# Cross-attention scores as three products of high and low halves

## The chip, the cores and the metric

The kernel runs on one core of one Trainium2 chip. The metric is device time in microseconds (us): the median of the runs of one launch of the whole program. In the views PE is TensorE (matmuls), PEld its weight loads, DVE is VectorE, ACT is ScalarE, POOL is GpSimd, SP is SyncE (it issues most of the DMAs).

## The reference, cut to what matters

One transformer block with cross-attention and a mixture of experts, on 8 sequences of 112 tokens of width 512 (896 tokens), each with a context of 375 rows. The self- and cross-attention parts share one shape of computation:

```python
q  = ln(fp8_linear(ln(x), wq));   k  = ln(fp8_linear(ln(x), wk));   v = fp8_linear(ln(x), wv)
core = softmax(q k^T / sqrt(128)) v           # 16 heads, 8 groups of keys and values, 112 x 112 scores
qx = ln(fp8_linear(ln(x), wqx))               # 16 heads of width 128
kx, vx = split(ctx @ w_kv_x);  kx = ln(kx)    # 8 groups of keys and values from the context
xout = softmax(qx kx^T / sqrt(128)) vx        # 112 x 375 scores for each head: the cross scores
y = fp8_round(concat(core, xout)) @ wproj     # then the gate, the residual, and 8 experts, 2 for each token
```

The change is in `qx kx^T`, and in buffers around it.

## The kernel before, in words

**Work and tiles.** The 16 heads are cut into 4 groups of 4 heads (`GP`, written `g`, 0 to 3). In each group there are 8 sequences (`u`, 0 to 7). A position `(g, u)` stands for the attention of sequence `u` in group `g`: 32 positions. The tokens come in only 7 tiles of 128 rows (`TJ`), so positions with `u` = 7 project no queries and keys of their own (`has_tile`). For one position and its 4 heads there are 4 cross scores: `score_cross(t, h)`, h = 0 to 3, each a matmul of 112 stationary columns (queries `qxT`) by 375 moving columns (context keys `kxT`), in f32. A pair of heads shares one set of keys: h = 0, 1 use `kxT[:, 0]`, h = 2, 3 use `kxT[:, 1]`. An f32 matmul is two records in the trace. Other big matmuls hold f32 numbers cut into a rounded high half and a low rest (type fp32r, tiles `..._hi` and `..._lo`), and each such matmul is one record.

**Steps.** `passes` runs one `step(s, t, ...)` after the other. In a step TensorE makes the six projections of position `s` and the attention of the position `t` before it, interleaved in an order written out by hand for every engine; each engine runs its own list in order and waits on semaphores. There are ordinary steps (`s` with `u` = 1 to 6), the `"new"` steps (`s` = `(g, 0)`, a new group), and `last_step` (`s` = `(g, 7)`, `t` = `(g, 6)`), with lists of their own. The lists of an ordinary step:

- TensorE (L902): project 0, turn 0, turn 1, project 1, turn 2, turn 3, project 2, score_self, score_cross 0 and 1, turn 4, project 3, turn_self, turn_cross 0, score_cross 2, turn_cross 1, score_cross 3, project 4, outputs 0, turn_cross 2 and 3, project 5, outputs 1. `turn` transposes queries and keys into PSUM (turn 1 the cross queries, turn 3 and 4 the two sets of context keys); `turn_cross` transposes exponentials. `turn_cross` 1 needs the bank that VectorE's `take_self` frees (`bank_free`, L802).
- ScalarE (L695): turned 0 (from PSUM to `qT`), take 0, turned 1 (to `qxT`, L647 and L648), turned 2, c_high 0, turned 3 (to `kxT`, L640), take 1, c_high 1, exp_self, exp_cross 0 and 1 (L664), turned 4, take 2, c_high 2, take 3, exp_cross 2 and 3, and so on. `c_high` (L581) rounds a third of the context to `c_hi`.
- VectorE (L1171): sums 0 (L1078), max_self (L1093), max_cross 0 and 1 (L1107), norm_self (L1099, L1101), norm_cross 0 and 1 (L1113, then L1115 twice), take_self (L1121), sums 1, take_cross 0 (L1126), max_cross 2, ...
- GpSimd (L532): c_low 0 (L529: `c_lo = c_raw - c_hi`, as soon as ScalarE has made that `c_hi`), rstd 0 (L516, L523), c_low 1, rstd 1, c_low 2, ...
- SyncE (L437): the loads of the context of a coming position, and the store of a finished position's rounded results (`Results.store`).

In the steps before and at a change of group VectorE and ScalarE also cut the next group's weights (`w_low` L434, `w_low_half` L971, `w_high` L576).

After the attention comes the output projection and the experts (`projected_experts`), which the change touches only through the tile `results`.

Of the kernel before, what the change touches and what calls it, by code (L numbers as in the profile page):

```python
# [25 lines left out]
P = 128  # L26
# [3 lines left out]
KB = D // P  # L30
# [150 lines left out]
class Results:  # L181
# [3 lines left out]
    def __init__(self, c, sb, sem, catd):  # L185
        self.catd = catd
        self.held = sb(c, "results", [P, 4 * 8 * T], BF16)
        *self.y, self.e, self.cat = (self.held[:, k * 8 * T:(k + 1) * 8 * T] for k in range(4))
        self.ya_done = sem(c, "ya_done")
        self.rnd = sem(c, "rnd_chain")  # L190
        self.ct_done = sem(c, "ct_done")
        self.stored = sem(c, "cat_out")
# [13 lines left out]
    def rounded(self, v, t):  # L206
        v.wait_ge(self.rnd, 3 * t + 2)
        y = self.y[t % 2]
        v.tensor_tensor(y[:, :], y[:, :], self.e[:, :], ALU.add).then_inc(self.rnd, 1)
        v.wait_ge(self.rnd, 3 * t + 3)  # L210
        v.wait_ge(self.stored, 16 * (t + 1))
        v.tensor_tensor(self.cat[:, :], y[:, :], self.e[:, :], ALU.subtract).then_inc(self.ct_done, 1)

    def store(self, sp, t):
        sp.wait_ge(self.ct_done, t + 1)
        sp.dma_start(self.catd[t], self.cat[:, :]).then_inc(self.stored, 16)
# [60 lines left out]

def tr_no(pos, n):

    return TR0 + 77 * pos[0] + 10 * pos[1] + n + 1 - (0 if has_tile(pos) else 3)  # L280
# [11 lines left out]
def attention(nc, c, sb, ps, sem, x, vecs, scalars, smooth, ctxT, wproj, catd, vec, scal, gate,  # L292
# [22 lines left out]
    sqx = sb(c, "sqx", [P, 2 * HD], BF16)  # L315
    re = sb(c, "re", [P, 4, 2, P], BF16)
    st = sb(c, "st", [P, TJ, 6])
# [6 lines left out]
    smr = sb(c, "smr", [P, GP, 8])  # L324
    work = sb(c, "work", [P, HP * TC + 2 * NC * 256 + NC * HP * T])
    pcross = work[:, 0:HP * TC].rearrange("p (h c) -> p h c", h=HP)
    at = HP * TC
# [4 lines left out]
    ss = sb(c, "ss", [P, 16])  # L332
    va = sb(c, "va", [P, 16])
    rs = sb(c, "rs", [P, 16])
# [3 lines left out]
    kxT = sb(c, "kxT", [P, 2, TC])  # L338
# [51 lines left out]
    sx_rdy = sem(c, "sx_rdy")  # L390
    mx_done = sem(c, "mx_done")
# [45 lines left out]
    def _(sp):  # L437
# [18 lines left out]
        sp.dma_start(smr[:, :, :], smooth).then_inc(vec_in, 16)  # L456
# [9 lines left out]
        for gp in range(GP):  # L466
# [19 lines left out]
            with sp.Fori(2, B) as b:  # L486
                for k in range(NC):
                    load_c(s0 + b, b, k)
                results.store(sp, s0 + b - 2)

    @block.gpsimd
    def _(pool):
# [4 lines left out]
        pool.wait_ge(pool_self, 3)  # L497
# [60 lines left out]
    def _(act):  # L558
# [71 lines left out]
        def turned(t, n):  # L630
# [8 lines left out]
            if n >= 3:  # L639
                act.activation(kxT[:, n - 3, :], turn_bank(n)[:, 0:TC], ACT.Identity, bias=b,  # L640
                               scale=w).then_inc(t_done, 1)
                return
# [17 lines left out]
        def exp_cross(t, h):  # L660
            act.wait_ge(mx_done, 4 * (lin(t) + 1) + h + 1)
            act.wait_ge(tr_rdy, tr_no(before(t), 6 + h))
            act.wait_ge(nx_done, 4 * lin(t) + h + 1)
            act.activation(pcross[0:T, h, :], p_cross[0:T, h % 2, 0:TC], ACT.Exp,  # L664
                           bias=nmax[0:T, 4 + h:5 + h], accum_out=lsum[0:T, 4 + h:5 + h]).then_inc(ex_done, 1)
# [29 lines left out]
        def step(s, t, g, change, k):  # L695
# [11 lines left out]
            if not A and Q: turned(t, 4)  # L707
            if A: take(s, 1)
            if A: c_high(s, 1)
# [3 lines left out]
            if A and Q: turned(t, 4)  # L713
# [42 lines left out]
    def _(pe):  # L756
# [18 lines left out]
        def project(s, j, g=None):  # L775
# [13 lines left out]
            else:  # L789
# [62 lines left out]
        def turn_cross(t, h):  # L852
            pe.wait_ge(nx_done, 4 * (lin(t) + 1) + h + 1)
            bank_free(t, 6 + h)
            for k in range(NC):
                m = pe.transpose(p_tr[0:CT, 1 - h % 2, k * T:(k + 1) * T], pcross[0:T, h, k * CT:(k + 1) * CT],  # L856
# [21 lines left out]
        def last_step(s, t):  # L878
# [5 lines left out]
            project(s, 3)  # L884
            turn(t, 3)
# [16 lines left out]
        def step(s, t, g, change, k):  # L902
# [45 lines left out]
    def _(v):  # L948
# [75 lines left out]
        def constants():  # L1024

            link(v.reciprocal(smi[:, :, :], smr[:, :, :]))
# [62 lines left out]

        def max_self(t):  # L1090
# [19 lines left out]
        def norm_cross(t, h):  # L1110
# [4 lines left out]
            v.tensor_scalar(pcross[0:T, h, :], pcross[0:T, h, :], linv[0:T, 4 + h:5 + h], None,  # L1115
# [22 lines left out]
        def last_step(s, t, g, change):  # L1138

            if change == "keys": w_low_half(g, 1, 0)  # L1140
            max_self(t)
# [5 lines left out]
            norm_cross(t, 1)  # L1147
            take_self(t)
# [22 lines left out]
        def step(s, t, g, change, k):  # L1171
# [885 lines left out]
```

## Time and profile before

| what | value |
|---|---|
| median of 3 runs | 1150.24 us (1149.46 to 1151.94) |
| the profiled execution: its time | 1153.25 us |
| the profiled execution: span, first to last instruction | 1151.5 us |
| TensorE busy | 1092.3 us, 95% of the span |
| VectorE busy | 779.6 us, 68% |
| ScalarE busy | 698.5 us, 61% |
| GpSimd busy | 505.0 us, 44% |
| granted TensorE clock, mean | 0.977 |

The attention takes the first 797 us or so, the output projection and the experts the rest. A timeline row reads: start in us from the span's first instruction, length in us, engine, line, operation, output tile <- input tiles, shapes, count of merged instructions, and in brackets the engine's idle time before it with what ended it.

### The profile page before, as it was taken

What the parts mean: (1) busy time and instruction counts of PE and PEld (TensorE: products, weight loads), DVE (VectorE), ACT (ScalarE), POOL (GpSimd) and SP (SyncE); (2) the same over time, 40 slices, a digit from 0 to 9 for tenths busy, and PEclk for the clock granted to TensorE, in tenths of its full rate; (3) what the DMA queues carried; (4) which work ended last, traced back from release to release, by engine and by line L of the source; (5) the groups of instructions that cost most, each with busy time, mean ns of one, the idle gap of its engine ahead of it and who ended that gap; (6) DMA issues with size and microseconds to landing.
All of it is one profiled execution on the core that took longest, in us unless ns stands there. A gap on an engine that the chain in (4) does not pass through costs nothing. (4 is left out here: it accounts for less than half of the span.)

```text
span 1151.5 us, 19576 instructions
## 1 busy us (share of the span) xinstructions
PE 1092.3 (95%) x5681; PEld 896.0 (78%) x5681; DVE 779.6 (68%) x1569; ACT 698.5 (61%) x2034; POOL 505.0 (44%) x576
## 2 busy tenths in 40 slices
PE   4599999999999999999999999998999789999996
PEld 3488788888888788888888888886888667777885
DVE  7998986977776887777697766677454884655000
ACT  7668878666878856888867656762231324334432
POOL 3445565445544454445544544542000225565432
PEclk8799999999999999999999999998999889999999
DMA  7221111142111214111114111112944347673220
GB/s 264 98 76 45 52 36 45 36 152 91 44 37 44 61 36 181 45 53 37 43 36 145 53 44 40 45 31 83 339 161 164 127 150 216 182 235 105 52 45 1
DMA packets 52820, 107.41 MB, mean 93 GB/s; under 512 B 6064, under 2 KB 27056, under 8 KB 51184
## 3 DMA queue, kind: packets, MB, share of 16 engines
q1 hardware_dynamic: 48016, 97.00, 25.7%
q0 software_dynamic: 4704, 9.18, 3.6%
q8 instruction: 50, 0.82, 0.3%
q14 instruction: 50, 0.41, 0.1%
HBM read 91.48 MB, written 16.52 MB: 94 GB/s over the span
## 5 line engine op out<-in xcount | busy, mean ns | idle before, releaser
L529 POOL TENSOR_TENSOR c_lo<-c_raw,c_hi 128x500 fp32r<-128x500 f32 x96 | 123.7, 1289 | 194.2 <-ACT c_hi L581 194.2
L523 POOL TENSOR_TENSOR rs<-va,mhalf 125x2 f32<-125x2 f32 (+1 forms) x180 | 200.7, 1115 | 14.2 <-POOL va L516 0.2
L516 POOL TENSOR_TENSOR va<-ss,epst 125x2 f32<-125x2 f32 (+1 forms) x180 | 60.6, 336 | 179.7 <-DVE ss L1078 101.5
L798 PE MATMUL bank<-w_hi,c_hi 128*125 128x512 f32 x384 | 120.0, 434 | 9.3 <-ACT w_hi L576 8.3
L771 PE MATMUL bank<-w_hi,xqs 128*128 128x512 f32 (+2 forms) x464 | 111.0, 361 | 11.4 <-DVE xqs L1070 11.4
L798 PE MATMUL bank<-w_lo,c_hi 128*125 128x512 f32 x384 | 105.4, 396 | 0.1
L798 PE MATMUL bank<-w_hi,c_lo 128*125 128x512 f32 x384 | 105.4, 396 | 0.0
L664 ACT ACTIVATE work<-bank,nmax 112x375 f32<-112x375 f32 x128 | 73.6, 584 | 46.7 <-DVE nmax L1107 46.7
L771 PE MATMUL bank<-w_lo,xqs 128*128 128x512 f32 (+2 forms) x464 | 101.0, 340 | 0.1
L842 PE MATMUL bank<-kxT,qxT 128*112 128x375 f32 x256 | 97.9, 484 | 0.0
L798 PEld LDWEIGHTS bank<-w_hi,c_hi 128*125 128x125 f32 x384 | 67.0, 188 | 27.6 <-issue 8.5
L771 PEld LDWEIGHTS bank<-w_hi,xqs 128*128 128x128 f32 (+1 forms) x464 | 73.7, 189 | 17.9 <-issue 12.0
L798 PEld LDWEIGHTS bank<-w_hi,c_lo 128*125 128x125 f32 x384 | 71.7, 187 | 18.5
L798 PEld LDWEIGHTS bank<-w_lo,c_hi 128*125 128x125 f32 x384 | 71.4, 186 | 18.8 <-DVE w_lo L434 0.8
L771 PEld LDWEIGHTS bank<-w_lo,xqs 128*128 128x128 f32 (+1 forms) x464 | 75.5, 187 | 11.4 <-DVE w_lo L434 0.8
L873 PE MATMUL bank<-work 125*128 125x224 f32 x384 | 83.2, 352 | 0.0
L1133 DVE TENSOR_TENSOR results<-bank,smg 128x448 bf16<-128x448 f32 x64 | 39.8, 622 | 53.2 <-PE bank L873 53.2
L626 ACT ACTIVATE nkx<-bank 125x256 f32<-125x256 f32 x96 | 38.8, 405 | 58.6 <-PE bank L798 58.6
L873 PEld LDWEIGHTS bank<-work 125*128 125x128 f32 x384 | 72.7, 190 | 0.4
L1107 DVE TENSOR_REDUCE nmax<-bank 112x1 f32<-112x375 f32 x128 | 69.1, 542 | 4.0 <-PE bank L842 1.3
L1523 POOL DMA_INDIRECT out<-p_cat,of_row x21 | 45.5, 2167 | 58.5 <-ACT p_cat L1627 43.4
L856 PEld LDWEIGHTS bank<-ident,work 112*125 112x125 f32 x384 | 52.2, 189 | 19.5 <-issue 13.6
(274 smaller groups left out, 2812.6 us busy)
## 6 DMA issues: line engine op xcount, KB each, us to landing
c_raw<-in_ctxT SPq DMA_DIRECT2D x96, 250.0 KB, 2.6
shared<-in_w_in SPq DMA_DIRECT2D x13, 1024.0 KB, 9.1
shared<-in_wproj SPq DMA_DIRECT2D x32, 256.0 KB, 4.5
raw_g<-in_Wg SPq DMA_DIRECT2D x8, 1024.0 KB, 6.5
raw_u<-in_Wu SPq DMA_DIRECT2D x8, 1024.0 KB, 6.1
raw_d<-in_Wd SPq DMA_DIRECT2D x8, 1024.0 KB, 5.5
cat_scratch<-results SPq DMA_DIRECT2D x32, 224.0 KB, 2.0
shared<-cat_scratch SPq DMA_DIRECT2D x2, 1792.0 KB, 9.0
```

The lines of the kernel that those rows point to most:

```text
L516: pool.tensor_tensor(va[0:rows, lo:hi], ss[0:rows, lo:hi], epst[0:rows, lo:hi], ALU.add).then_inc(va_done, 1)
L523: pool.tensor_tensor(rs[0:rows, lo:hi], va[0:rows, lo:hi], mhalf[0:rows, lo:hi], ALU.pow).then_inc(rs_done, 1)
L529: pool.tensor_tensor(flat(c_lo[:, k, :, :]), flat(c_raw[:, k, :, :]), flat(c_hi[:, k, :, :]).bitcast(F32), ALU.subtract).then_inc(cl_done, 1)
L664: act.activation(pcross[0:T, h, :], p_cross[0:T, h % 2, 0:TC], ACT.Exp, bias=nmax[0:T, 4 + h:5 + h], accum_out=lsum[0:T, 4 + h:5 + h]).the ...
L771: m = pe.matmul(out, xqs[:, n, k, 0:rows], (w_hi, w_lo)[i // KB][:, k, lo:lo + w], start=(i == 0), stop=(i == 2 * KB - 1))
L798: m = pe.matmul(bank[0:CT, :], a[:, ch, k, :], w[:, k, CKX:CV], start=(i == 0), stop=(i == 3 * KB - 1))
L842: pe.matmul(p_cross[0:T, h % 2, 0:TC], qxT[:, t[1] % 2, h, :], kxT[:, h // HPG, :], start=True, stop=True).then_inc(sx_rdy, 1)
L856: m = pe.transpose(p_tr[0:CT, 1 - h % 2, k * T:(k + 1) * T], pcross[0:T, h, k * CT:(k + 1) * CT], ident[0:T, 0:T])
L873: m = pe.matmul(out[:, HPG * T:2 * HPG * T], valx[0:CT, par, k, g * P:(g + 1) * P], flat(pcrossT[0:CT, k, HPG * g:HPG * (g + 1), :]), star ...
L1107: v.tensor_reduce(nmax[0:T, 4 + h:5 + h], p_cross[0:T, h % 2, 0:TC], AX, ALU.max, negate=True).then_inc(mx_done, 1)
L1133: v.tensor_tensor(results.y[lin(t) % 2][:, g * 4 * T:(g + 1) * 4 * T].rearrange("p (a t) -> p a t", t=T), out_bank(t, g)[:, 0:4 * T].rearr ...
L1523: pool.indirect_dma_start(out=tokens[:, :], out_offset=bass.IndirectOffsetOnAxis(ap=of_row[:, 1, i:i + 1], axis=0), in_=y[:, i % 2, :], in ...
```

## The change

For every position outside the first group that has a token tile of its own (`has_halves`: g = 1 to 3, u = 0 to 6, so 21 positions and 84 of the 128 cross scores), VectorE cuts the cross queries and each set of context keys into a rounded high half and a low rest, and a cross score becomes three fp32r matmuls added up in PSUM: high by high, low by high, high by low, over 376 columns (one column of zeros more). The other 44 scores stay f32. `kxT` holds one set of keys in place of two, so that turned 4 waits until the first set has been cut (or used). For these positions turn 4 moves ahead of score_self on TensorE, turned 4 ahead of exp_self on ScalarE, and c_high 1 from before exp_self to behind exp_cross 1. In `last_step` (all four) turn 3 moves into project 3, behind the first 4 of its 12 matmuls. The exponentials have 2 buffers in place of 4; the rounded results stay in `y` and are stored from there, without the tile `cat`; some small tiles share space; SyncE's loop over positions is unrolled. The diff, cut:

```diff
--- before
+++ after
@@ class Results
-        self.held = sb(c, "results", [P, 4 * 8 * T], BF16)
-        *self.y, self.e, self.cat = (self.held[:, k * 8 * T:(k + 1) * 8 * T] for k in range(4))
+        self.held = sb(c, "results", [P, 6 * FF], BF16)
+        *self.y, self.e = (self.held[:, k * 8 * T:(k + 1) * 8 * T] for k in range(3))
+        self.rest = self.held[:, 3 * 8 * T:6 * FF]
...
-        v.wait_ge(self.stored, 16 * (t + 1))
-        v.tensor_tensor(self.cat[:, :], y[:, :], self.e[:, :], ALU.subtract).then_inc(self.ct_done, 1)
+        v.tensor_tensor(y[:, :], y[:, :], self.e[:, :], ALU.subtract).then_inc(self.ct_done, 1)
...
-        sp.dma_start(self.catd[t], self.cat[:, :]).then_inc(self.stored, 16)
+        sp.dma_start(self.catd[t], self.y[t % 2][:, :]).then_inc(self.stored, 16)
@@ has_tile
+def has_halves(pos):
+    return pos[0] > 0 and has_tile(pos)
+
+def halves_no(pos, n):
+    return 6 * (TJ * (pos[0] - 1) + pos[1]) + n + 1
@@ attention: buffers (sqx, ss, va, rs move into results.rest, st into work; smr is smi)
-    work = sb(c, "work", [P, HP * TC + 2 * NC * 256 + NC * HP * T])
-    pcross = work[:, 0:HP * TC].rearrange("p (h c) -> p h c", h=HP)
+    work = sb(c, "work", [P, 2 * TC + 2 * NC * 256 + NC * HP * T])
+    pcross = work[:, 0:2 * TC].rearrange("p (h c) -> p h c", h=2)
...
-    kxT = sb(c, "kxT", [P, 2, TC])
+    kxT = sb(c, "kxT", [P, TC + 1])
+    qx_hi = sb(c, "qx_hi", [P, HP, T], F32R)
+    qx_lo = sb(c, "qx_lo", [P, HP, T], F32R)
+    kx_hi = sb(c, "kx_hi", [P, TC + 1], F32R)
+    kx_lo = sb(c, "kx_lo", [P, TC + 1], F32R)
@@ sync (SyncE)
-            with sp.Fori(2, B) as b:
+            for b in range(2, B):
@@ gpsimd: one memset more at the start, of kxT[:, TC:TC + 1]
@@ scalar: turned, exp_cross, step
             if n >= 3:
-                act.activation(kxT[:, n - 3, :], turn_bank(n)[:, 0:TC], ACT.Identity, bias=b,
+                if n == 4 and has_halves(t):
+                    act.wait_ge(halves, halves_no(t, 3))
+                elif n == 4:
+                    act.wait_ge(sx_rdy, 4 * (lin(t) + 1) + 2)
+                act.activation(kxT[:, 0:TC], turn_bank(n)[:, 0:TC], ACT.Identity, bias=b,
...
-            act.wait_ge(tr_rdy, tr_no(before(t), 6 + h))
+            act.wait_ge(tr_rdy, tr_no(before(t), 8 + h) if h < 2 else tr_no(t, 4 + h))
...
             if Q: turned(t, 3)
-            if not A and Q: turned(t, 4)
             if A: take(s, 1)
-            if A: c_high(s, 1)
+            early = Q and has_halves(t)
+            if early: turned(t, 4)
+            elif A: c_high(s, 1)
             if Q: exp_self(t)
             if Q: exp_cross(t, 0)
             if Q: exp_cross(t, 1)
-            if A and Q: turned(t, 4)
+            if early: c_high(s, 1)
+            elif Q: turned(t, 4)
             if A: take(s, 2)
@@ tensor: project, score_cross, last_step, step
-        def project(s, j, g=None):
+        def project(s, j, g=None, t=None):
...
+                    if i == KB and t is not None: turn(t, 3)
                     if i == KB: pe.wait_ge(cl_done, 3 * (lin(s) + 1) + ch + 1)
...
-            pe.matmul(p_cross[0:T, h % 2, 0:TC], qxT[:, t[1] % 2, h, :], kxT[:, h // HPG, :],
-                      start=True, stop=True).then_inc(sx_rdy, 1)
+            out, par, kh = p_cross[0:T, h % 2, 0:TC + 1], t[1] % 2, h // HPG
+            if not has_halves(t):
+                pe.matmul(out[:, 0:TC], qxT[:, par, h, :], kxT[:, 0:TC], start=True, stop=True).then_inc(sx_rdy, 1)
+                return
+            q_hi, q_lo = qx_hi[:, h, :], qx_lo[:, h, :]
+            pe.wait_ge(halves, halves_no(t, 2 + 2 * kh))
+            pe.matmul(out, q_hi, kx_hi[:, :], start=True, stop=False)
+            pe.matmul(out, q_lo, kx_hi[:, :], start=False, stop=False)
+            pe.wait_ge(halves, halves_no(t, 3 + 2 * kh))
+            pe.matmul(out, q_hi, kx_lo[:, :], start=False, stop=True).then_inc(sx_rdy, 1)
...
             turn(t, 2)
-            project(s, 3)
-            turn(t, 3)
+            project(s, 3, None, t)
             score_self(t)
...
-            if not A: turn(t, 4)
-            if not A: score_self(t)
             if A: project(s, 2, g)
-            if A and Q: score_self(t)
+            if Q and has_halves(t): turn(t, 4)
+            if Q: score_self(t)
             if Q: score_cross(t, 0)
             if Q: score_cross(t, 1)
-            if A and Q: turn(t, 4)
+            if Q and not has_halves(t): turn(t, 4)
@@ vector
+        def halves_of_queries(t):
+            if not has_halves(t):
+                return
+            whole = flat(qxT[:, t[1] % 2, :, :])
+            v.wait_ge(t_done, td_no(t, 1))
+            v.wait_ge(sx_rdy, 4 * lin(t) + 4)
+            v.tensor_copy(flat(qx_hi[:, :, :]), whole).then_inc(halves, 1)
+            v.wait_ge(halves, halves_no(t, 0))
+            v.tensor_tensor(flat(qx_lo[:, :, :]), whole, flat(qx_hi[:, :, :]).bitcast(F32),
+                            ALU.subtract).then_inc(halves, 1)
+
+        def halves_of_keys(t, kh):
+            if not has_halves(t):
+                return
+            v.wait_ge(t_done, td_no(t, 3 + kh))
+            v.wait_ge(sx_rdy, 4 * lin(t) + 4 + 2 * kh)
+            v.tensor_copy(kx_hi[:, :], kxT[:, :]).then_inc(halves, 1)
+            v.wait_ge(halves, halves_no(t, 2 + 2 * kh))
+            v.tensor_tensor(kx_lo[:, :], kxT[:, :], kx_hi[:, :].bitcast(F32),
+                            ALU.subtract).then_inc(halves, 1)
...
-                v.wait_ge(results.ct_done, lin(t) - 1)
+                v.wait_ge(results.stored, 16 * lin(t))
...
@@ vector: last_step
+            halves_of_queries(t)
+            halves_of_keys(t, 0)
             max_self(t)
...
             norm_cross(t, 1)
+            halves_of_keys(t, 1)
             take_self(t)
@@ vector: step
+            if Q: halves_of_queries(t)
+            if Q: halves_of_keys(t, 0)
             if Q: max_self(t)
             if Q: max_cross(t, 0)
             if Q: max_cross(t, 1)
+            if Q: halves_of_keys(t, 1)
             if change == "new": results.rounded(v, lin(before(t)))
```

## Rows read from the trace of the kernel before

**Rows 1.** Stretch of group 1: busy time per engine, clock, DMA share (windows).

```profile
250.00:437.00 187.00, 185.99 (x1024) 155.04 (x1024) 143.38 (x302) 143.23 (x463) 91.76 (x114) 1.00 0.21 66
```

**Rows 2.** Timeline of TensorE, ordinary step with t = (2, 2).

```profile
486.32 0.63 PE L771 MATMUL bank<-w_hi,xqs 128*112 128x256 f32 x4
...
487.26 0.94 PE L835 MATMUL bank<-kT,qT 128*112 128x112 f32 x8
488.05 1.43 PE L842 MATMUL bank<-kxT,qxT 128*112 128x375 f32 x4
489.31 0.49 PE L825 MATMUL bank<-ident,nkx 125*128 125x125 f32 x3
489.55 1.18 PE L798 MATMUL bank<-w_hi,c_hi 128*125 128x512 f32 x4
490.56 1.08 PE L798 MATMUL bank<-w_hi,c_lo 128*125 128x512 f32 x4
...
492.42 0.55 PE L849 MATMUL bank<-ident,pself 112*112 112x112 f32 x4
...
493.13 0.80 PE L842 MATMUL bank<-kxT,qxT 128*112 128x375 f32 x2
```

**Rows 3.** Timeline of ScalarE, same step.

```profile
485.09 0.54 ACT L648 ACTIVATE qxT<-bank,vec 128x192 f32<-128x192 f32 x1
...
486.17 0.66 ACT L581 ACTIVATE c_hi<-c_raw 128x500 fp32r<-128x500 f32 x1
486.68 0.71 ACT L640 ACTIVATE kxT<-bank,vec 128x375 f32<-128x375 f32 x1
...
488.91 0.35 ACT L656 ACTIVATE pself<-bank,nmax 112x112 f32<-112x112 f32 x1
...
491.24 0.23 ACT L664 ACTIVATION_READ_ACCUMULATOR work<-bank,nmax 112x1 f32 x1
```

**Rows 4.** Timeline of VectorE, same step.

```profile
485.55 0.68 DVE L1078 TENSOR_REDUCE ss<-sq 128x4 f32<-128x512 f32 x1
488.25 0.62 DVE L1093 TENSOR_REDUCE nmax<-bank 112x4 f32<-112x448 f32 x1 [2.02 <-PE bank L835]
...
490.60 0.62 DVE L1101 TENSOR_TENSOR pself<-pself,linv 112x448 f32<-112x448 f32 x1
...
491.70 0.74 DVE L1115 TENSOR_SCALAR work<-work,linv 112x375 f32<-112x375 f32 x2
```

**Rows 5.** Timeline of GpSimd, same step.

```profile
486.91 1.26 POOL L529 TENSOR_TENSOR c_lo<-c_raw,c_hi 128x500 fp32r<-128x500 f32 x1 [5.54 <-ACT c_hi L581]
```

**Rows 6.** Timeline of VectorE, ordinary step with t = (3, 5).

```profile
746.67 0.63 DVE L1093 TENSOR_REDUCE nmax<-bank 112x4 f32<-112x448 f32 x1 [2.81 <-PE bank L835]
```

**Rows 7.** Timeline of all engines, last step with t = (3, 6).

```profile
771.61 0.23 ACT L664 ACTIVATION_READ_ACCUMULATOR work<-bank,nmax 112x1 f32 x1
...
772.40 1.50 DVE L1115 TENSOR_SCALAR work<-work,linv 112x375 f32<-112x375 f32 x1
772.43 1.26 POOL L529 TENSOR_TENSOR c_lo<-c_raw,c_hi 128x500 fp32r<-128x500 f32 x1 [4.55 <-ACT c_hi L581]
...
774.58 0.44 PE L856 MATMUL bank<-ident,work 112*125 112x112 f32 x2
```

**Rows 8.** Groups by line, VectorE: count, busy us, mean ns, idle before.

```profile
L1982 DVE CAST hi_u<-raw_u 128x2048 fp32r<-128x2048 f32 x7 | 8.5, 1220 | 0.0
```

**Rows 9.** Timeline of all engines, in the experts.

```profile
939.50 1.56 POOL L1517 TENSOR_TENSOR results<-results 128x512 f32<-128x512 f32 x1 [12.39 <-ACT results L1605]
939.85 2.29 DVE L1982 CAST hi_d<-raw_d 128x2048 fp32r<-128x2048 f32 x1
```

**Rows 10.** Timeline of all engines, last step with t = (1, 6).

```profile
391.77 1.09 PE L798 MATMUL bank<-w_hi,c_lo 128*125 128x512 f32 x4
...
392.05 0.42 DVE L1087 TENSOR_TENSOR nkx<-nkx,rs 125x256 f32<-125x256 f32 x1
...
393.11 2.28 DVE L971 TENSOR_TENSOR w_lo<-shared,w_hi 128x1024 fp32r<-128x1024 f32 x1
```

More of the change, by code:

```diff
@@ L314, in attention @@
     sq = sb(c, "sq", [P, 2, 512])
-    sqx = sb(c, "sqx", [P, 2 * HD], BF16)
+    sqx = results.rest[:, 0:2 * HD]
     re = sb(c, "re", [P, 4, 2, P], BF16)
-    st = sb(c, "st", [P, TJ, 6])
     mv = sb(c, "mv", [P, TJ, 2])
@@ L323, in attention @@
     xof = sb(c, "xof", [P, 4, KB])
-    smr = sb(c, "smr", [P, GP, 8])
-    work = sb(c, "work", [P, HP * TC + 2 * NC * 256 + NC * HP * T])
-    pcross = work[:, 0:HP * TC].rearrange("p (h c) -> p h c", h=HP)
-    at = HP * TC
+    work = sb(c, "work", [P, 2 * TC + 2 * NC * 256 + NC * HP * T])
+    pcross = work[:, 0:2 * TC].rearrange("p (h c) -> p h c", h=2)
+    at = 2 * TC
     valx = work[:, at:at + 2 * NC * 256].rearrange("p (a k n) -> p a k n", a=2, k=NC)
@@ L331, in attention @@
     xs = work[:, 0:TJ * D].rearrange("p (j d) -> p j d", j=TJ)
-    ss = sb(c, "ss", [P, 16])
-    va = sb(c, "va", [P, 16])
-    rs = sb(c, "rs", [P, 16])
+    st = work[:, TJ * D:TJ * D + TJ * 6].rearrange("p (j n) -> p j n", j=TJ)
+    ss, va, rs = (results.rest[:, 2 * HD + 32 * n:2 * HD + 32 * (n + 1)].bitcast(F32) for n in range(3))
     qT = sb(c, "qT", [P, 2, HP, T])
@@ L390, in attention @@
     sx_rdy = sem(c, "sx_rdy")
+    halves = sem(c, "cross_halves")
     mx_done = sem(c, "mx_done")
@@ L455, in _ @@
         sp.dma_start(scal[:, :], scalars.partition_broadcast(P)).then_inc(vec_in, 16)
-        sp.dma_start(smr[:, :, :], smooth).then_inc(vec_in, 16)
+        sp.dma_start(smi[:, :, :], smooth).then_inc(vec_in, 16)
         for j in range(1, TJ):
@@ L496, in _ @@
         pool.memset(epst[:, :], EPS).then_inc(pool_self, 1)
-        pool.wait_ge(pool_self, 3)
+        pool.memset(kxT[:, TC:TC + 1], 0.0).then_inc(pool_self, 1)
+        pool.wait_ge(pool_self, 4)
         pool.affine_select(out=ident[:, :], in_=ident[:, :], compare_op=ALU.not_equal, fill=1.0,
@@ L661, in exp_cross @@
             act.wait_ge(mx_done, 4 * (lin(t) + 1) + h + 1)
-            act.wait_ge(tr_rdy, tr_no(before(t), 6 + h))
+            act.wait_ge(tr_rdy, tr_no(before(t), 8 + h) if h < 2 else tr_no(t, 4 + h))
             act.wait_ge(nx_done, 4 * lin(t) + h + 1)
-            act.activation(pcross[0:T, h, :], p_cross[0:T, h % 2, 0:TC], ACT.Exp,
+            act.activation(pcross[0:T, h % 2, :], p_cross[0:T, h % 2, 0:TC], ACT.Exp,
                            bias=nmax[0:T, 4 + h:5 + h], accum_out=lsum[0:T, 4 + h:5 + h]).then_inc(ex_done, 1)
@@ L855, in turn_cross @@
             for k in range(NC):
-                m = pe.transpose(p_tr[0:CT, 1 - h % 2, k * T:(k + 1) * T], pcross[0:T, h, k * CT:(k + 1) * CT],
+                m = pe.transpose(p_tr[0:CT, 1 - h % 2, k * T:(k + 1) * T], pcross[0:T, h % 2, k * CT:(k + 1) * CT],
                                  ident[0:T, 0:T])
@@ L1024, in constants @@
         def constants():
-            link(v.reciprocal(smi[:, :, :], smr[:, :, :]))
+            link(v.reciprocal(smi[:, :, :], smi[:, :, :]))
             for col in (V_KW, V_KB, V_KXW, V_KXB):
@@ L1114, in norm_cross @@
                 v.wait_ge(dv, CH * lin(t) + 2 + h // 2)
-            v.tensor_scalar(pcross[0:T, h, :], pcross[0:T, h, :], linv[0:T, 4 + h:5 + h], None,
+            v.tensor_scalar(pcross[0:T, h % 2, :], pcross[0:T, h % 2, :], linv[0:T, 4 + h:5 + h], None,
                             ALU.mult).then_inc(nx_done, 1)
```

## Prediction

> **What bounds the kernel now.** I read the busy shares first, then windows over whole groups, then one ordinary step engine by engine, then the places where GpSimd and VectorE overlap. In group 1 TensorE is busy 185.99 of 187 us at full granted clock (1.00, the 2.4 GHz level) [rows 1]; groups 2 and 3 look alike. A group has 8 steps, so a step takes 23.4 us on average, and in an ordinary one TensorE never pauses. So only two things count there: TensorE's own time, and any new wait of TensorE. VectorE (143 us of 187) and ScalarE have room on average, but they work inside TensorE's order: keys go from TensorE (turn 3) to ScalarE (`kxT`) and back to score_cross, with VectorE idle 2.02 us before max_self [rows 4]. The change puts VectorE into that path.
>
> **TensorE's own time.** Two f32 scores run from 488.05 to 489.31, so 0.63 us each [rows 2]. An fp32r pass over 512 columns takes (492.42 - 490.56) / 8 = 0.2325 us, one over 256 columns (487.26 - 486.32) / 8 = 0.1175 us [rows 2]. On the straight line between, 376 columns take 0.171 us; the two rows are the bounds. Three passes take 0.514 us, so a score gains 0.116 us (bounds 0.28 gained, 0.07 lost), 0.46 us for a position. The first four fp32r matmuls behind f32 transposes take 490.56 - 489.55 = 1.01 us, 0.08 more than 4 x 0.2325 [rows 2]. The new order has two more such changes of type for a position (around score 2): 0.16 us. Net gain: 0.30 us for a position. The extra weight loads run under the passes, as those of the 512-column rows do.
>
> One rule would give more. The Trainium skill ("FP8 and Floating Point Precision", TensorE Precision Notes) counts true f32 as four passes, so three would cost three quarters: by it a score takes 0.47 us and 84 scores save 13 us. The rows give 84 x 0.116 = 9.7 us before the changes of type, and I keep them.
>
> **VectorE's new work.** A cast of 448 or 376 columns lies near the normalisation of 375 columns, a pair of which takes 0.74 us [rows 4], some 0.4 each; I take 0.45 and 0.41 (from below: 2048 columns in 1.22 us, 0.6 ns a column, make 0.22 [rows 8]). A subtraction of 448 columns is like L1101, 0.62 us [rows 4]; 376 columns 0.54. A position adds 0.45 + 0.62 + 2 x (0.41 + 0.54) = 2.97 us to a VectorE that is busy 143.38 / 8 = 18 us of a step [rows 1]. It fits on average; the question is where it lands.
>
> **Where it collides.** A free pair of normalisations takes 0.74 us [rows 4]; in rows 7 the second one alone takes 1.50: GpSimd's c_low runs from 772.43 to 773.69, and the normalisation, started at 772.40, ends only at 773.90, 0.21 behind c_low's end. An fp32r cast is held likewise: 2.29 us in place of 1.22 beside GpSimd's product [rows 8, 9]. So a VectorE operation of these kinds that comes during c_low ends 0.21 us behind it. The Trainium skill ("SBUF — State Buffer", Who interferes with whom) states the cause as one port pair that is held for a whole instruction by whichever of the two starts first; the trace agrees on the holding.
>
> First collision, score 0. I follow one step. VectorE is free at 486.2 [rows 4] and has `qxT` since 485.63 [rows 3], so it casts the queries until 486.65 and subtracts until 487.27. c_low 0 wants to start at 486.91 [rows 5], waits until about 487.2, and ends at 488.45. `kxT` is done at 487.39 [rows 3]: the cast of the keys is held and ends at 488.66, the subtraction at 489.24. TensorE would be ready for score 0 at 488.05 + 0.24 (turn 4 now ahead of it) = 488.29, plus 0.08 for the change of type; its third pass would start at 488.71 and can't before 489.3 (0.05 for the signal). Cost 0.59 us. In 10 of the 18 ordinary steps VectorE is idle 2.8 us and not 2.0 [rows 6]; there the queries are done before c_low starts, which ends at 488.17 as before, the subtraction ends at 488.96, and the cost is 0.31 us.
>
> Second collision, turn_cross 1. c_high 1 now stands right behind exp_cross 1 on ScalarE, as c_high 2 does in the last step, so c_low 1 comes 0.59 us behind the end of exp_cross 1, as it does there (771.84 to 772.43 [rows 7]), just as VectorE reaches its second normalisation (0.56 behind, 772.40). take_self is behind it, and turn_cross 1 waits for take_self: 2.74 us behind the end of exp_cross 1 (774.58). When is that end? max_self can start only when the keys' subtraction is over: about 489.2 in place of 488.25 [rows 4], so its end is 489.8; exp_self starts at 489.85, exp_cross 1 ends 2.56 us later (491.47 - 488.91 [rows 3]) at 492.4, and turn_cross 1 starts at 495.15. TensorE would come there earlier: score 0 ends at 489.47, score 1 at 489.99, project 3 2.79 us later, turn_self and turn_cross 0 0.71 [rows 2], score 2 0.60: 494.1. Cost 1.05 us, the same in the 10 milder steps, where both sides come earlier. Behind turn_cross 1 the step has room again (project 4, 2.8 us).
>
> An ordinary step thus changes by -0.30 + 0.59 + 1.05 = +1.34 us (8 of them) or -0.30 + 0.31 + 1.05 = +1.06 us (10): +10.7 + 10.6 = +21.3 us.
>
> **The last steps.** Turn 3 inside project 3 comes at 391.77, but its `nkx` is scaled only at 392.47, behind the weights' subtraction [rows 10]: 0.75 us of waiting, in three of the four (t = (0, 6), (1, 6), (2, 6)); it gives nothing back in the first, which has no halves. In (1, 6) and (2, 6) the queries' halves stand behind `w_low_half`, which ends at 395.39 [rows 10], so the keys' cast ends at 396.7 and the subtraction at 397.3, against score 0 ready at 395.7: 1.3 us. There the second keys' halves stand behind norm_cross 1, which is held as in rows 7, so score 2 waits some 1.2 us and turn_cross 1 0.4, of which 0.5 was waited before. Sum 3 us each, 6 us; (3, 6) has only this second part, 1.2; (0, 6) 0.8. Together +8 us.
>
> **Costed at nothing.** Two buffers for exponentials: exp_cross 2 waits for turn_cross 0, which TensorE has done before score 2 anyway. One `kxT`: turned 4 waits for the keys' subtraction (489.24), then runs in front of exp_self, which waits for max_self longer still (489.78); in other positions it stands behind exp_cross 1 as before. Storing from `y`: smoothed waits for the store of two positions back, over a step old. c_high 1 later: c_low 1 ends near 494.3, and project 4, which starts behind score 3, needs it near 497. SyncE's unrolled loop has the same waits and loads, far ahead of use. GpSimd's memset of one column is over long before the first scores. Should one of these covers fail, its price is a wait of some tenths of a us in each of 21 positions.
>
> **Sum.** 21.3 + 8 = +29.3 us: 1153.25 becomes 1182.5 for the profiled execution, and 1179.5 for the median, which lies 3.0 us lower.
>
> **The rivals.** (a) The second collision doesn't happen. In rows 7 c_low starts 0.03 us behind the second normalisation and yet goes first; a tenth of a us decides. Without it an ordinary step changes by +0.01 or +0.29, 2.4 us in all, and with the last steps +10.4: 1160.6. By the rule of the Trainium skill's page named above, taken on the recorded starts, VectorE would be first and (a) would hold; the row shows the other order. (b) The keys' cast is not held, as a 376-column cast is short; then only the second collision is left: 18 x (1.05 - 0.30) = 13.5, and the last steps some 7: 1171. (c) The other side, faster: neither holds, because c_low 0 is over when `kxT` is done (it would have to end 0.8 us sooner) and VectorE is a tenth of a us ahead at the second normalisation. Then 18 x 0.30 = 5.4 us come off, the last steps cost between 1 (if turn 3's wait is covered) and 5: 1146 to 1150. For it speaks that VectorE has 2 us idle just there; against it, that c_low runs in just that idle time [rows 4, 5]. (d) The passes run at f32 pace, two records each: +84 x 1.26 = 106 us; the fp32r rows speak against it.
>
> **How the numbers follow.** Both collisions 0.46 (1179.5, own range 1170 to 1187: every second hold milder, or 0.3 us more in each step), (a) 0.12, (b) 0.11, (c) 0.28, (d) and the like 0.03. A measurement here tells about 0.2%, 2.3 us, from no change; (c) lies partly within it, so I give faster 0.20, same 0.09, slower 0.71. The range, 1148 to 1187, leaves out the part of (c) below 1148 and what lies above 1187. The bounds of the pass (0.28 gained, 0.07 lost a score) would move the sum by -14 or +16 us, but 376 columns lie between both rows, and I don't widen for them.
>
> **What would show it.** Right: fp32r passes on score_cross every 0.17 us; gaps of TensorE of 0.3 to 0.6 us in front of the third pass of score 0 (or the first) with VectorE's cast 0.7 to 1.3 us long beside c_low; a second normalisation of 1.4 us beside c_low 1, and a gap of 1 us before turn_cross 1 put down to take_self; groups that take 8 to 10 us longer. Wrong: groups 2 us shorter, casts of 0.4 us throughout, no TensorE gap before turn_cross 1. What would make me wrong in size is the place of c_low 1 against the normalisations, two in three of the 29 us.

## The result, and the profile after

The changed kernel takes 1175.51 us (median; 1174.24 to 1178.12) against 1150.14 us for the kernel before on the same chip: ratio 1.0221, interval 1.0205 to 1.0237, slower by 25.4 us. The forecast was 1179.5 us (1148 to 1187), slower. In the profiled execution the stretch from the first score_self to that of position (3, 7) grew from 719.21 to 744.50 us, by 25.3 us, so all of the loss lies in the attention. (From there to the last instruction it took from 364.1 to 368.5 us in the profiles of this study, with the same work in each; a difference of 2 us there says nothing.)

TensorE lost what [rows 1] showed of it: group 1's stretch of the changed kernel is no longer full. The columns are those of [rows 1].

```profile
250.00:437.00 187.00, 177.55 (x1002) 151.61 (x1001) 164.04 (x327) 140.29 (x452) 90.77 (x108) 1.00 0.20 65
```

TensorE is busy 177.55 us of 187 at full granted clock, where it was busy 185.99; VectorE rose from 143.38 to 164.04, some 2.6 us for each of the 8 steps, part of it time in which it is held, as shown below. VectorE is still idle for 23 us of the 187, so it is not the bound on average. The groups of instructions of the changed kernel's page say which wait it is (busy, mean ns of one, idle time before and what ended it):

```profile
L885 PE MATMUL bank<-ident,work 112*125 112x112 f32 x384 | 60.3, 280 | 18.8 <-DVE pselfT L1171 17.6
```

17.6 us of TensorE's idle time stand before turn_cross and end with take_self (L1171, its output is `pselfT`). The timeline of TensorE in the step with t = (2, 2) answers to [rows 2]:

```profile
499.54 0.95 PE L856 MATMUL bank<-kT,qT 128*112 128x112 f32 x8
500.62 0.40 PE L869 MATMUL bank<-kx_hi,qx_hi 128*112 128x376 f32 x1
500.86 0.33 PE L870 MATMUL bank<-kx_hi,qx_lo 128*112 128x376 f32 x1
501.11 0.42 PE L872 MATMUL bank<-kx_lo,qx_hi 128*112 128x376 f32 x1
501.37 0.33 PE L869 MATMUL bank<-kx_hi,qx_hi 128*112 128x376 f32 x1
501.54 0.33 PE L870 MATMUL bank<-kx_hi,qx_lo 128*112 128x376 f32 x1
501.71 0.33 PE L872 MATMUL bank<-kx_lo,qx_hi 128*112 128x376 f32 x1
501.89 1.10 PE L819 MATMUL bank<-w_hi,c_hi 128*125 128x512 f32 x4
...
505.76 0.33 PE L872 MATMUL bank<-kx_lo,qx_hi 128*112 128x376 f32 x1
507.02 0.55 PE L885 MATMUL bank<-ident,work 112*125 112x112 f32 x3 [0.93 <-DVE pselfT L1171]
```

Read the starts, since the ends overlap: the passes of score 1 start every 0.17 us (501.37, 501.54, 501.71, and the next matmul at 501.89), as forecast. Score 0 has pauses that the view does not mark as gaps: its first pass starts 1.08 us behind score_self, its third 0.25 behind the second, and score 1 only 0.26 behind that third. Then 0.93 us before turn_cross 1. VectorE in the same step answers to [rows 4]:

```profile
498.10 0.38 DVE L1124 CAST qx_hi<-qxT 128x448 fp32r<-128x448 f32 x1
498.52 0.63 DVE L1126 TENSOR_TENSOR qx_lo<-qxT,qx_hi 128x448 fp32r<-128x448 f32 x1
499.38 1.09 DVE L1135 CAST kx_hi<-kxT 128x376 fp32r<-128x376 f32 x1 [0.24 <-ACT kxT L658]
500.51 0.55 DVE L1137 TENSOR_TENSOR kx_lo<-kxT,kx_hi 128x376 fp32r<-128x376 f32 x1
...
502.55 0.35 DVE L1135 CAST kx_hi<-kxT 128x376 fp32r<-128x376 f32 x1
...
504.53 1.82 DVE L1165 TENSOR_SCALAR work<-work,linv 112x375 f32<-112x375 f32 x2
506.27 0.61 DVE L1171 COPY pselfT<-bank 112x448 f32<-112x448 f32 x1
```

and GpSimd, answering to [rows 5]:

```profile
498.87 1.39 POOL L543 TENSOR_TENSOR c_lo<-c_raw,c_hi 128x500 fp32r<-128x500 f32 x1 [5.42 <-ACT c_hi L595]
...
504.88 1.25 POOL L543 TENSOR_TENSOR c_lo<-c_raw,c_hi 128x500 fp32r<-128x500 f32 x1 [2.96 <-ACT c_hi L595]
```

Both forecast collisions are there. The keys' cast takes 1.09 us beside c_low 0 and 0.35 us when it runs alone (the second one, 502.55); c_low 0 ends at 498.87 + 1.39 = 500.26, the cast at 499.38 + 1.09 = 500.47, 0.21 behind it. The pair of normalisations takes 1.82 us beside c_low 1, in place of 0.74 [rows 4], and take_self stands behind it. The subtraction ends at 501.06, and the third pass starts at 501.11: that was the forecast's signal of 0.05 us.

One step is different by itself. In t = (3, 2) c_low 1 comes at the same point, but VectorE and GpSimd show

```profile
700.44 0.74 DVE L1165 TENSOR_SCALAR work<-work,linv 112x375 f32<-112x375 f32 x2
701.17 0.62 DVE L1171 COPY pselfT<-bank 112x448 f32<-112x448 f32 x1
```

```profile
700.79 1.50 POOL L543 TENSOR_TENSOR c_lo<-c_raw,c_hi 128x500 fp32r<-128x500 f32 x1 [2.96 <-ACT c_hi L595]
```

Here the pair takes 0.74 us, and it is GpSimd's operation that is long (1.50 in place of 1.26). TensorE has no gap before turn_cross 1, and the step lasts 23.90 us where its neighbours last 24.9. Rival (a) of the forecast thus happened in 1 of 18 steps.

### The profile page after: what moved, and what is told of

Read it like the earlier page. It is cut to its first block and busy times, and to the rows that moved or that the text cites. A ratio compares the mean times of both kernels' runs of the same rounds, so it can differ in the third digit from the quotient of the medians.

```text
span 1174.0 us, 19558 instructions
## 1 busy us (share of the span) xinstructions
PE 1092.9 (93%) x5765; PEld 909.1 (77%) x5765; DVE 861.7 (73%) x1695; ACT 699.2 (60%) x2034; POOL 513.7 (44%) x577
## 3 DMA queue, kind: packets, MB, share of 16 engines
q1 hardware_dynamic: 48016, 97.00, 25.4%
## 5 line engine op out<-in xcount | busy, mean ns | idle before, releaser
L537 POOL TENSOR_TENSOR results<-results,mhalf 125x2 f32<-125x2 f32 (+1 forms) x180 | 206.3, 1146 | 14.1
L530 POOL TENSOR_TENSOR results<-results,epst 125x2 f32<-125x2 f32 (+1 forms) x180 | 61.3, 341 | 140.6 <-ACT results L616 73.7
L819 PE MATMUL bank<-w_hi,c_hi 128*125 128x512 f32 x384 | 112.3, 414 | 8.1 <-ACT w_hi L590 6.7
L885 PE MATMUL bank<-ident,work 112*125 112x112 f32 x384 | 60.3, 280 | 18.8 <-DVE pselfT L1171 17.6
L1165 DVE TENSOR_SCALAR work<-work,linv 112x375 f32<-112x375 f32 x128 | 72.5, 607 | 2.3
```

The source lines that it names most:

```text
L530: pool.tensor_tensor(va[0:rows, lo:hi], ss[0:rows, lo:hi], epst[0:rows, lo:hi], ALU.add).then_inc(va_done, 1)
L537: pool.tensor_tensor(rs[0:rows, lo:hi], va[0:rows, lo:hi], mhalf[0:rows, lo:hi], ALU.pow).then_inc(rs_done, 1)
L1165: v.tensor_scalar(pcross[0:T, h % 2, :], pcross[0:T, h % 2, :], linv[0:T, 4 + h:5 + h], None, ALU.mult).then_inc(nx_done, 1)
```

## The experiments

Theory A is the forecast's: c_low 0 holds the keys' cast, c_low 1 holds the second normalisation, and VectorE's lists in the last steps add waits. "Step" below is the time from one score_self to the next; before it was 23.85 us in ordinary steps, after it is 24.9 (the 10 milder, "early" steps of the forecast, save (3, 2)) or 25.0 (the 8 "late" ones; one of them, (1, 1), 25.29). The figures are those of u = 0 to 4; for u = 5 the time runs into a last step.

**c_high 1 behind take 2.** The second collision alone is taken away, by making c_low 1 start later:

```diff
             if Q: exp_cross(t, 1)
-            if early: c_high(s, 1)
-            elif Q: turned(t, 4)
+            if Q and not early: turned(t, 4)
             if A: take(s, 2)
+            if early: c_high(s, 1)
```

> c_high 1 moves on ScalarE from behind exp_cross 1 to behind take 2, so GpSimd's c_low 1 starts about 0.8 us later, when VectorE is past its second normalisation. Theory A (VectorE is held by GpSimd's c_low): the 0.94 us gap of TensorE before turn_cross 1 goes away in the 17 steps that show it, 16 us less, about 1159.5 us. Rival B (VectorE is late because of its own 2.6 us more of work for a position): the gap stays, no change, 1175 us. Rival C (the smaller buffers cause the waits): no change.

Measured: 1159.56 us (1158.97 to 1162.15), ratio 1.0094 [1.0071, 1.0117], 16 us less than the changed kernel. Timelines of TensorE and of VectorE, t = (2, 2):

```profile
497.78 0.33 PE L872 MATMUL bank<-kx_lo,qx_hi 128*112 128x376 f32 x1
498.04 0.55 PE L885 MATMUL bank<-ident,work 112*125 112x112 f32 x3
```

```profile
496.54 0.74 DVE L1165 TENSOR_SCALAR work<-work,linv 112x375 f32<-112x375 f32 x2
```

No marked gap before turn_cross 1; the pair of normalisations is free. Some 0.1 us of waiting is left there (0.26 between the two starts shown, where a pass takes 0.17); the run with both moves shows what it is. Steps last 23.89 and 24.01 us.

**c_high 0 ahead of turned 0.** The first collision alone is taken away: c_low 0 is over when the keys come.

```diff
+            early = Q and has_halves(t)
+            if early: c_high(s, 0)
...
-            if A: c_high(s, 0)
+            if A and not early: c_high(s, 0)
```

> c_high 0 moves on ScalarE ahead of turned 0, into ScalarE's idle time, so that c_low 0 is over before the keys reach VectorE. Theory A: the keys' cast takes 0.35 us in place of 0.96 to 1.09, the passes of score 0 follow at 0.17 us, and 18 ordinary steps lose 0.35 to 0.5 us each, 7 us together, about 1168 us; the gap before turn_cross 1 stays. Rival B: no change, since VectorE's work is the same.

Measured: 1168.55 us (1167.37 to 1170.2), ratio 1.0166 [1.0143, 1.0189], 7 us less than the changed kernel. TensorE, t = (2, 1):

```profile
471.46 0.95 PE L857 MATMUL bank<-kT,qT 128*112 128x112 f32 x8
472.18 0.40 PE L870 MATMUL bank<-kx_hi,qx_hi 128*112 128x376 f32 x1
...
478.40 0.55 PE L886 MATMUL bank<-ident,work 112*125 112x112 f32 x3 [0.94 <-DVE pselfT L1172]
```

Score 0 starts 0.72 us behind score_self in place of 1.08, while the wait before turn_cross 1 stays. All ordinary steps last 24.47 us, early or late.

**Both moves.**

> Both moves together. Theory A: the ordinary steps come to 23.85 - 0.30 = 23.55 us, what is left of the slowdown is the last steps' 3 to 6 us less the gain of 5.4: about 1152 us. Rival B: about 1175 us.

Measured: 1149.51 us (1148.83 to 1151.2), ratio 1.000 [0.999, 1.001]. TensorE, t = (2, 2):

```profile
487.75 0.48 PE L847 MATMUL bank<-ident,nkx 125*128 125x125 f32 x3
488.07 0.95 PE L857 MATMUL bank<-kT,qT 128*112 128x112 f32 x8
488.79 0.40 PE L870 MATMUL bank<-kx_hi,qx_hi 128*112 128x376 f32 x1
489.03 0.33 PE L871 MATMUL bank<-kx_hi,qx_lo 128*112 128x376 f32 x1
489.20 0.33 PE L873 MATMUL bank<-kx_lo,qx_hi 128*112 128x376 f32 x1
489.37 0.34 PE L870 MATMUL bank<-kx_hi,qx_hi 128*112 128x376 f32 x1
489.55 0.33 PE L871 MATMUL bank<-kx_hi,qx_lo 128*112 128x376 f32 x1
489.72 0.33 PE L873 MATMUL bank<-kx_lo,qx_hi 128*112 128x376 f32 x1
489.89 1.09 PE L820 MATMUL bank<-w_hi,c_hi 128*125 128x512 f32 x4
...
493.75 0.33 PE L873 MATMUL bank<-kx_lo,qx_hi 128*112 128x376 f32 x1
494.02 0.55 PE L886 MATMUL bank<-ident,work 112*125 112x112 f32 x3
```

and take_self on VectorE, same step:

```profile
493.25 0.62 DVE L1172 COPY pselfT<-bank 112x448 f32<-112x448 f32 x1
```

Ordinary steps last 23.48 us, 0.37 less than before, without a marked gap. One small wait is left: turn_cross 1 starts 0.27 us behind the last pass of score 2 (494.02 - 493.75), where a pass takes 0.17, and 0.15 us behind the end of take_self (493.87). It starts 0.15 us behind the end of take_self in every ordinary step of the kernel before, of the changed one and of this one, so take_self still sets it, and 0.10 us of TensorE's gain goes there. The moved c_low 0 meets other work now: in 10 steps it holds the scaling of `nkx` (1.49 us in place of 0.41), and TensorE does not wait for that. From here the prices of the two collisions can be read by subtraction. In the steps of the first experiment the first collision costs 0.41 us (early, 23.89 - 23.48) or 0.53 (late, 24.01 - 23.48), in those of the second the second collision 0.99 (24.47 - 23.48), and in the changed kernel both together 1.4 to 1.5: they add up. So do the attention stretches of the profiles, 17.1 and 7.9 us shorter with one move and 25.5 with both; the medians give 16.0, 7.0 and 26.0.

**No halves, the rest of the change stays.** `has_halves` is false everywhere: all scores f32, but with the smaller buffers, one `kxT` and turn 3 inside project 3.

> has_halves is false for every position: all 128 scores stay f32, and the rest of the change stays (smaller buffers, results stored from y, unrolled loop, turn 3 inside project 3). The predicted steps say: buffers cost nothing, turn 3 waits 0.6 us for its nkx in three last steps: 1150 to 1152 us. Rival C: a good part of the 25 us stays, above 1160 us.

Measured: 1152.2 us (1151.56 to 1153.68), ratio 1.0019 [1.0008, 1.003]. Ordinary steps last 23.83 us, as before. By the ratio it is 2.2 us slower than before; 1.8 are the wait of turn 3 for `nkx`, 0.6 us in three last steps, and the attention of the profile is 1.1 us longer (720.35 us). The buffers cost nothing that shows.

**The kernel before with one move.** No halves at all; c_high 1 goes behind exp_cross 1 in the 18 ordinary positions.

```diff
-            if A: c_high(s, 1)
+            late = Q and t[0] > 0 and has_tile(t)
+            if A and not late: c_high(s, 1)
...
             if Q: exp_cross(t, 1)
+            if late: c_high(s, 1)
```

> The kernel before, f32 scores and no halves, with one move alone: c_high 1 from before exp_self to behind exp_cross 1 for the 18 ordinary positions outside the first group. Theory A (the second collision is made by that move, whatever VectorE does besides): the second normalisation is held to about 1.5 us in these positions, take_self is late and TensorE waits before turn_cross 1. Without the keys' halves TensorE reaches turn_cross 1 some 0.5 us later against exp_cross 1 than in the changed kernel, so the wait is smaller, some 0.4 to 0.5 us, 18 times: about +8 us, 1157.5 (1155 to 1167). Rival (VectorE's own halves make the wait, the place of c_high 1 does not matter without them): 1149.5 us, ratio 1.000.

Measured: 1158.69 us (1157.52 to 1161.05), ratio 1.0076 [1.006, 1.0093]. TensorE, VectorE and GpSimd, t = (2, 0):

```profile
448.08 0.55 PE L858 MATMUL bank<-ident,work 112*125 112x112 f32 x3 [0.29 <-DVE pselfT L1123]
```

```profile
445.56 1.83 DVE L1117 TENSOR_SCALAR work<-work,linv 112x375 f32<-112x375 f32 x2
```

```profile
445.92 1.27 POOL L529 TENSOR_TENSOR c_lo<-c_raw,c_hi 128x500 fp32r<-128x500 f32 x1 [2.64 <-ACT c_hi L581]
```

The held pair and the wait appear without a single cast or subtraction of halves. A step lasts 24.29 us, 0.44 more, 18 times: 7.9 us of the 8.7. The rival, that VectorE's own new work makes this wait, falls: the move alone does. In the changed kernel it is dearer (0.99 in place of 0.44), since TensorE is ready for turn_cross 1 earlier: 1.64 us behind the end of exp_cross 1 in place of 2.29, with turn 4 ahead of score_self and shorter scores.

**The last steps mended too**, on top of both moves (ScalarE's turned 4 goes ahead of exp_self there and c_high 2 behind take 3 as well):

```diff
@@ VectorE, step
-            if change == "queries": w_low(g, 0)
             if A: scale(s, 5)
+            if change == "queries": w_low(g, 0)
@@ VectorE, last_step
-            if change == "keys": w_low_half(g, 1, 0)
+            if change == "keys" and not has_halves(t): w_low_half(g, 1, 0)
...
-            if change == "keys": results.rounded(v, lin(before(t)))
+            halves_of_keys(t, 1)
+            if change == "keys" and not has_halves(t): results.rounded(v, lin(before(t)))
...
-            halves_of_keys(t, 1)
...
             max_cross(t, 3)
+            if change == "keys" and has_halves(t): results.rounded(v, lin(before(t)))
...
             if change == "keys":
+                if has_halves(t): w_low_half(g, 1, 0)
@@ TensorE, last_step
-            project(s, 3, None, t)
+            project(s, 3, None, t if has_halves(t) else None)
+            if not has_halves(t): turn(t, 3)
+            if has_halves(t): turn(t, 4)
```

> The kernel with both ScalarE moves, and besides in the last steps: VectorE scales nkx ahead of cutting the weights, the queries' and both keys' halves come ahead of the second half of the weights and of norm_self, rounded comes behind max_cross 3, ScalarE's turned 4 stands ahead of exp_self and c_high 2 behind take 3, TensorE's turn 4 ahead of score_self, and turn 3 goes inside project 3 only where a position has halves. Theory A (the waits that are left are those of VectorE's lists in the last steps): TensorE's gaps of 0.6 us before turn 3 go in three steps, of 1.07 + 0.89 + 0.2 us before the scores and turn_cross in two, of 0.9 us in one; 7 us less than the kernel with both moves, so about 1142.5 us, ratio 0.994 to the kernel before. Rival (VectorE has no room there, so the waits come back at the weights or later in the step): 1147 to 1150 us, with new gaps of TensorE behind the group change.

Measured: 1146.31 us (1143.08 to 1150.39), ratio 0.997 [0.9955, 0.9985]: faster than before by 3.7 us, where 7 less than with both moves were expected. The profile shows less: the attention took 717.82 us, 1.2 less than with both moves (719.03). The runs of this kernel spread over 7 us, and the profiled one, 1150.39 us, is the longest of the 12, so where the rest of the gain lies is not shown. Timelines of TensorE and of VectorE at the change to group 2:

```profile
419.85 0.60 PE L882 MATMUL bank<-ident,pself 112*112 112x112 f32 x4 [1.66 <-DVE pself L1157]
```

```profile
406.74 2.35 DVE L1004 TENSOR_TENSOR w_lo<-shared,w_hi 128x1024 fp32r<-128x1024 f32 x2
```

The two steps that run up to and on from the score_self of (1, 6) came down, from 22.12 + 22.69 to 21.61 + 20.99 us. But the moved half of the weights is now cut at 406.74, VectorE has no pause from there to the next step's scores, and that step rose from 25.00 to 27.77 us, with a gap of 1.66 us before turn_self where 0.54 was. So both answers hold: the waits were those of the lists, and around a change of group they come back (2.8 us for the 2.2 gained), because VectorE is short of time there. What the profile keeps comes from the other last steps: 1.7 us around (3, 6) and 0.6 around (0, 6).

**rounded later in the steps that begin a group**, on top of that:

```diff
-            if change == "new": results.rounded(v, lin(before(t)))
...
             if Q: max_cross(t, 3)
+            if change == "new": results.rounded(v, lin(before(t)))
```

> The kernel with both ScalarE moves and the reordered last steps, and besides, in the steps that begin a group, rounded (two operations of VectorE, 1.42 us together) behind max_cross 3 in place of ahead of norm_self. Theory A (VectorE's list, not its load, makes the gap of 1.66 us before turn_self at each of two group changes and of 0.54 us at the first): the gaps shrink by 1.4, 1.4 and 0.54 us, 3.3 us less than without the move, 1143 us, ratio 0.994 to the kernel before. Rival (VectorE is short of time around the group change, so that the wait goes to turn_cross or to the next step): 1146 us, no change.

Measured: 1146.2 us (1143.21 to 1149.91), ratio 0.997 [0.9957, 0.9983]. In the profile the steps behind the two changes fell from 27.77 to 26.4 us, the first rose by 0.4, and the attention took 715.75 us in place of 717.82; the medians are the same. The part behind the attention varies by more than these 2 us, so the times don't decide between the two answers. The trace shows some of each: at the two changes the gap before turn_self fell from 1.66 to 1.00 us and not by 1.4, and new gaps of 0.29 and 0.32 us stand before turn_cross in the same step.

**The same without halves.**

> The same kernel with all scores in f32 and no halves (the last steps then have the lists of the kernel before, and scale of nkx and rounded stay moved). It prices the halves themselves. Theory A (with every wait gone the halves are worth 0.35 us a step): 18 x 0.35 = 6.3 us more than with halves from the ordinary steps, and nearly nothing from the last steps: 1148.5 us, 1.6 us below the kernel before from the gap at the group changes. Rival (the gain of the run with halves comes from the reordering alone): the same time as with halves, 1143 us.

Measured: 1150.38 us (1149.46 to 1152.38), ratio 1.0009 [0.9999, 1.0018]. This kernel with f32 scores is no faster than the kernel before, so the two moves that it keeps (the scale of `nkx` and rounded) are not the gain. Halves, with the order that goes with them, are worth 1150.38 - 1146.2 = 4.2 us by the medians, 719.48 - 715.75 = 3.7 us of attention in the profiles. The ordinary steps, in which TensorE has no marked gap with or without halves, give 18 x 0.35 = 6.3 us, and the step from (3, 6) on 1.1; the steps behind the changes of group take 0.4, 1.5 and 1.5 back. The reordered last steps with f32 scores were not run, so halves and order are told apart in the ordinary steps alone.

## Why the prediction was right, term by term

The likeliest case came about, by both of its mechanisms; its size was 4 us too high, and two errors in TensorE's own gain (below) nearly cancel. The terms, measured from the steps of the kernel with both moves and those with one; the last steps are what is left of the kernel with both moves:

| term | forecast, us | measured, us |
|---|---|---|
| TensorE's gain, 18 steps | -5.4 (0.30 each) | -6.7 (0.37 each, with the wait that is left) |
| first collision | 7.8 (8 x 0.59, 10 x 0.31) | 8.3 (8 x 0.53, 10 x 0.41) |
| second collision | 18.9 (18 x 1.05) | about 17 (17 x 0.99) |
| last steps | 8 | 6.5 (719.03 - 719.21 + 6.7) |
| sum | 29.3 | 25.1; the attention grew by 25.3 |

**The gain.** The passes came at the interpolated 0.17 us, so that the four scores of a position gain 0.46 us, as worked out. The mis-sized term is the 0.16 us for "two more such changes of type". The new order has one more: f32 to fp32r was gone through twice a step before, ahead of projects 3 and 4, and is now gone through three times, ahead of scores 0, 2 and 3. And the price of 0.08 us was a misreading of starts. The first fp32r matmul behind f32 ones is recorded before the time of the last of these is over (at 489.55 in [rows 2], where three transposes of 0.32 us together end at 489.63), and the second follows later than usual (0.24 us in place of 0.17 in score 0), which makes that good. That 0.32 us is what turn 4 takes where an f32 matmul follows (488.07 - 487.75, both moves). In [rows 2] turn 4 and the four matmuls behind it take 490.56 - 489.31 = 1.25 us, which is 0.32 + 4 x 0.2325: nothing is left for the change of type.

What took the 0.1 us in its place is the wait for take_self before turn_cross 1 that is left with both moves: 0.46 - 0.10 = 0.36 against 0.37 measured. The forecast did not have it, and that the net gain came near 0.30 is in part luck. The rule of the Trainium skill that the forecast set against the rows ("FP8 and Floating Point Precision", TensorE Precision Notes: four f32 passes, so three would take three quarters of the time) would have given an estimate of 0.63 - 0.47 = 0.16 a score; the trace gives 0.63 - 3 x 0.172 = 0.11, and the measurement decides.

**The first collision** is shown by its removal (7 us) and by the cast's two durations. The third pass does wait for the subtraction, but a pass that has waited costs another 0.09 us: score 1 follows it after 0.26 us and not 0.17. That makes the early steps dearer than forecast: the third pass comes 0.3 us later there than with both moves (1.43 and 1.13 us behind score_self), as worked out, and 0.09 come on top. In the late steps c_low 0 ended 1.62 us behind the start of `kxT` on ScalarE (500.26 - 498.64), where 1.77 was worked out. The forecast let c_low 0 wait for the queries' subtraction and then take its whole 1.26 us; it ended 1.11 us behind that subtraction (500.26 - 499.15).

**The second collision** is shown three times: by its removal (16 us), by its making in the kernel before (8.7 us, no halves at all), and by t = (3, 2), where GpSimd lost. Forecast 1.05, measured 0.99 a step. TensorE's whole wait before turn_cross 1 is 507.02 - 505.76 - 0.17 = 1.09 us; the other 0.10 is the wait that stays.

**The last steps.** The wait of turn 3 was 0.6 us and not 0.75, three times. The timelines of TensorE and VectorE in the last step of group 1 show the rest:

```profile
399.66 0.54 PE L846 MATMUL bank<-ident,nkx 125*128 125x125 f32 x3 [0.60 <-DVE nkx L1114]
...
403.93 0.40 PE L869 MATMUL bank<-kx_hi,qx_hi 128*112 128x376 f32 x1 [1.08 <-DVE kx_hi L1135]
...
410.15 0.40 PE L869 MATMUL bank<-kx_hi,qx_hi 128*112 128x376 f32 x1 [0.88 <-DVE kx_hi L1135]
...
411.26 0.55 PE L885 MATMUL bank<-ident,work 112*125 112x112 f32 x3 [0.20 <-DVE pselfT L1171]
```

```profile
400.26 2.29 DVE L998 TENSOR_TENSOR w_lo<-shared,w_hi 128x1024 fp32r<-128x1024 f32 x1
402.48 0.38 DVE L1124 CAST qx_hi<-qxT 128x448 fp32r<-128x448 f32 x1
...
408.00 1.73 DVE L1165 TENSOR_SCALAR work<-work,linv 112x375 f32<-112x375 f32 x2
409.66 0.34 DVE L1135 CAST kx_hi<-kxT 128x376 fp32r<-128x376 f32 x1
```

1.08, 0.88 and 0.20 us stand where 1.3, 1.2 and 0.4 were forecast, in the places named and for the reasons named: the halves wait behind the weights' subtraction, and the second keys behind the held normalisations. The forecast's sum for these steps, 8 us, came out at 6.5.

**Costed at nothing** were the buffers, the single `kxT` and the store from `y`: the run without halves agrees, save for turn 3. The part that was not costed and came is the wait for take_self above.

**The rivals.** (a) held in one step of 18; (b) fell with the cast of 1.09 us; (c) needed both collisions to be absent: the kernel with both moves is that case, and it gave 1149.5 us, at the upper end of the 1146 to 1150 worked out for it, since all the last steps' waits stayed.

## What to carry to other kernels

Cutting f32 operands into halves on VectorE looks cheap by its busy share, and is dear where its operations meet GpSimd's: look in the profile for which GpSimd operations run in the idle time that the new work is to fill. Moving one instruction on an engine with room (c_high on ScalarE) moved the start of work on a second engine, held a third and stopped TensorE; such a move is to be followed through to the last engine, and can be tried by itself in the kernel before. A change that loses 25 us may hold a gain: two moves on ScalarE gave back 26 us, and the last steps' lists 3 us more by the medians (1.2 to 3.3 us in the attention of the profiles), to a version 0.3% faster than the kernel before. A gain on one engine counts only up to the next wait: in the ordinary steps 0.10 of TensorE's 0.46 us went into waiting for take_self. And a matmul's price is to be read from start to start over a whole run of matmuls, since the record of the first one behind another type starts early.

## What the runs showed of the hardware

**Who goes first is not told by the recorded starts.** In the changed kernel c_low 1's record starts 18 to 28 ns behind that of the second normalisation in the 18 ordinary steps. GpSimd went first in 17 of them; in t = (3, 2), at 27 ns, VectorE did; in t = (3, 0), at 28 ns, GpSimd. The Trainium skill ("SBUF — State Buffer", Who interferes with whom) gives the ports to whoever issues first, for the whole instruction. That one of the two is held until the other ends agrees in all 18; that the recorded start names the winner does not. With the second collision made in other kernels GpSimd went first in all 18 steps, at 22 to 24 ns. The second normalisation's record starts 0.08 us before the end of the first one's (504.86 against 504.94 in t = (2, 2)), so its start is hardly the moment at which it takes the ports; that is argued, not shown. What decides within these 30 ns is left open.

**The one that is held ends its own time behind the other, less 0.13 to 0.2 us.** Where GpSimd went first, VectorE's normalisation of 375 columns (0.4 us free) ended 210 to 217 ns behind c_low in all these kernels, and a cast of 376 columns (0.35 free) 0.21 us. That is no constant: the cast of 2048 columns in [rows 9] (1.22 us free) ended 1.08 us behind GpSimd (942.14 against 941.06), and a held c_low (1.26 us free) 1.11 us behind VectorE. So the forecast's "ends 0.21 us behind it" was right for operations of some 375 columns, the only ones that it used it for; to the held c_low 0 it gave the whole 1.26 us, 0.15 too much.

**After a wait the next matmul is late too**, at full granted clock: 0.09 us behind the third pass of score 0, as the starts show. It is not the accumulation alone that does it: behind the first transpose of turn_cross 1, which waited 0.93 us in t = (2, 2), the second starts 0.17 us later, where 0.11 is usual.
